# A matmul of zeros ahead of each visit's wait, taken out of the prologue of a graph network kernel

## The reference, cut to what matters

```python
def rgcn_conv(x, src, dst, etype, W, root, bias):      # layer 0, three times
    n = x.shape[0]
    seg = dst * R + etype                              # R = 5 relations
    agg = segment_sum(x[src], seg, n * R)
    cnt = segment_sum(ones, seg, n * R)
    agg = where(cnt > 0, agg / maximum(cnt, 1), 0).reshape(n, R, -1)
    return einsum('nrd,rdk->nk', agg, W) + x @ root + bias

# layer 1 (attention): sums of exp(-leaky_relu(s1[src] + s2[dst])) * h[dst] by src
# layer 2: sums of edge_weight * x[src] by dst, then a linear map
# layer 3: mean of edge_attr by dst, then an MLP
```

## Time and profile before

| | |
|---|---|
| median of 3 runs | 5415.35 us (5401.39 to 5419.33) |
| profiled execution | 5398.16 us |
| its span, first to last instruction | 5396.4 us |
| mean granted TensorE clock | 0.794 |
| TensorE matmuls busy | 3765.6 us (70%) |
| VectorE busy | 2663.4 us (49%) |
| GpSimd busy | 2356.5 us (44%) |
| ScalarE busy | 1163.5 us (22%) |

### The profile page before, as it was taken

One profiled execution on the slowest core, in us unless ns is written; L12 is line 12 of the kernel. 1 busy time (PEld: TensorE's weight loads), 2 busy tenths in 40 slices (PEclk: granted clock), 3 DMA queues, 4 the chain that ended last, 5 costly groups with the idle time before them and its releaser, 6 DMA issues.

```text
span 5396.4 us, 103191 instructions
## 1 busy us (share of the span) xinstructions
PE 3765.6 (70%) x20688; PEld 3046.7 (56%) x20691; DVE 2663.4 (49%) x6964; ACT 1163.5 (22%) x3868; POOL 2356.5 (44%) x2346
## 2 busy tenths in 40 slices
PE   4777677788888766666666776767676766757873
PEld 1333566666666655555555555656565655656762
DVE  7654454444444455545544544444444444892235
ACT  0122111121222111111222222222222222441112
POOL 0000465555555454545555555556555553003430
PEclk8999788888889877766766667887777776888886
DMA  2022333444444322222222223333333432436640
GB/s 73 32 66 75 103 108 114 117 120 118 119 126 133 110 55 55 55 58 64 76 76 74 77 82 104 109 109 108 104 105 107 111 107 67 170 134 176 179 118 12
DMA packets 478385, 526.90 MB, mean 98 GB/s; under 512 B 96596, under 2 KB 398238, under 8 KB 474670
## 3 DMA queue, kind: packets, MB, share of 16 engines
q1 hardware_dynamic: 252780, 246.52, 14.7%
q0 software_dynamic: 85824, 199.51, 13.8%
q10 hardware_dynamic: 139746, 80.46, 5.1%
HBM read 399.82 MB, written 126.39 MB: 98 GB/s over the span
## 4 chain that ended last, share of the span: by engine, by line
PE 31%; issue 25%; DMA 9%; DVE 9%; another core or an unknown queue 7%; POOL 6%; ACTq 4%; ACT 3%; DVEq 3%; SPq 2%; POOLq 1%
DMA msg_r<-y_tab,idx_r 7%; PE psum L1616 6%; POOL msg_r L635 6%; PE psum L1894 3%; PE psum L1689 2%; PE psum L1618 2%; PE psum L1804 1%; DVE shot_r L1151 1%; PE psum L1765 1%; PE psum L1805 1%; DVE h_t L1413 1%; ACT idx_r L712 1%; PE psum L1554 1%; PE psum L1542 1%
## 5 line engine op out<-in xcount | busy, mean ns | idle before, releaser
L635 POOL DMA_INDIRECT msg_r<-y_tab,idx_r x2160 | 2198.1, 1018 | 2327.9 <-issue 1115.5
L1616 PE MATMUL psum<-shot_r 128*128 128x200 f32 x2604 | 982.1, 478 | 404.8 <-issue 207.7
L1145 DVE SCALAR_TENSOR_TENSOR shot_r<-edge_f,win_base,iota 128x600 bf16<-128x600 f32 x434 | 366.3, 844 | 1437.3 <-remote 849.4
L712 ACT COPY idx_r<-row_i 128x1 int32 x2142 | 396.0, 191 | 1921.3 <-DMA msg_r<-y_tab,idx_r 1092.7
L1616 PEld LDWEIGHTS psum<-shot_r 128*128 128x128 f32 x2604 | 542.0, 258 | 438.4 <-issue 433.6
L1689 PE MATMUL psum<-hot_r,msg_r 128*128 128x128 f32 x2880 | 510.4, 320 | 162.1 <-DMA msg_r<-y_tab,idx_r 134.9
L1804 PE MATMUL psum<-msg_r,shot_r 128*128 128x128 f32 x1440 | 394.1, 364 | 305.4 <-DMA msg_r<-in_attr 103.7
L1689 PEld LDWEIGHTS psum<-hot_r,msg_r 128*128 128x128 f32 x2880 | 420.8, 219 | 231.4 <-DMA msg_r<-y_tab,idx_r 143.7
L1131 DVE TENSOR_SCALAR hot_r<-iota,edge_g 128x128 f32<-128x128 f32 x1602 | 446.4, 354 | 181.4 <-PE psum L1805 90.3
L1618 PEld LDWEIGHTS psum<-shot_r 128*100 128x100 bf16 x2604 | 430.2, 165 | 128.6 <-issue 20.3
L1804 PEld LDWEIGHTS psum<-msg_r,shot_r 128*128 128x128 f32 x1440 | 279.1, 241 | 375.2 <-issue 183.2
(11 more groups left out here) (315 smaller groups left out, 4746.5 us busy)
## 6 DMA issues: line engine op xcount, KB each, us to landing
msg_r<-in_attr SPq DMA_DIRECT2D x882, 64.0 KB
h_t<-count_tab SPq DMA_DIRECT2D x25, 1600.0 KB, 6.7
w_tab<-shot_r ACTq DMA_DIRECT2D x385, 100.0 KB
count_tab<-shot_r ACTq DMA_DIRECT2D x385, 100.0 KB
h_t<-w_tab SPq DMA_DIRECT2D x24, 1600.0 KB
msg_r<-y_tab,idx_r POOLq DMA_INDIRECT x2160
xn<-heavy_tab SPq DMA_DIRECT2D x76, 320.0 KB
y_tab<-y_s SPq DMA_DIRECT2D x25, 640.0 KB, 2.9
```

What stands on the lines that cost most here:

```text
L635: pool.indirect_dma_start(out=msg_r[:, q, 0:width], out_offset=None, in_=table, in_offset=bass.IndirectOffsetOnAxis(ap=idx_r[:, q:q + 1], ...
L712: nc.scalar.copy(idx_r[:, q:q + 1], of[:, q:q + COLS - U + 1][:, bass.ds(c0, 1)]).then_inc(s_idx[k], 1)
L1145: V.scalar_tensor_tensor(out=key_b, in0=of(KEY, KW), scalar=win_base[:, bass.ds(w, 1)], in1=to(KW), op0=ALU.subtract, op1=ALU.is_equal).th ...
L1616: T.matmul(win_ps, low_f[:, i, :], weighted_f[:, i, :], start=False, stop=False)
```

## The change

The one line in the visit loop that multiplies zeros into the open sums is taken out. It stood ahead of the wait and added 128 x 128 zeros by 500 columns of zeros to the sums of the window, so the result is unchanged. The opening and the closing matmul of each window stay.

```diff
                     clear(window)
                     with pe.Fori(v0, v1) as v:
                         slot = bounded(pe.snap(v % VD), 0, VD - 1, "it is a remainder")
-                        T.matmul(window, zeros_b[:, 0:P], zeros_b[:, 0:KEYS], start=False, stop=False)
                         pe.wait_ge(s_vis, v)
                         T.matmul(window, visit_r[:, bass.ds(slot, 1), 0:P].rearrange("p o n -> p (o n)"),
                                  visit_r[:, bass.ds(slot, 1), P:P + KEYS].rearrange("p o n -> p (o n)"),
                                  start=False, stop=False).then_inc(s_vfree, 1)
```

## The result

| | before | changed |
|---|---|---|
| median | 5402.92 us (19 runs) | 5450.51 us (19 runs) |
| ratio, 95% interval | | 1.0083 [1.0062, 1.0104] |
| profiled execution | 5398.16 us | 5475.73 us |
| prologue, L1542 of tile 0 to the transposition of the inverse counts | 455.3 us | 498.7 us |
| granted clock in it | 0.93 | 0.71 |

One of the 19 runs of the changed kernel took 5609.29 us at a mean clock of 0.595; it belongs to a slower state of the chip and is left out of the ratio.

What follows compares the result with a forecast made beforehand. TensorE's instruction issue was taken to bound the edited prologue's visits, VectorE those of window 0. Saving 3.2 us and losing 41.8 us in tables gave +38.6 us on 5415.35, so 5454 us; range 5426 to 5474.

Steps and rivals of the forecast that it cites:

- The issue price: Visit loop: each removed load and matmul of zeros saves 0.02 us of TensorE's queue, 3.2 us over 162 visits.
- The upper bound of 0.17: Visit loop: the most a visit could save, 0.32 us between loads less two address instructions; at most 27.5 us in all.
- Window 0: First window's 29 visits: VectorE's one-hot builds set the pace, 0.98 us a visit, so removal saves nothing there.
- The clock: Visits without zeros lose the full clock and nothing restores it before the next table; visits at half clock lose nothing.
- Rival A: Prologue: the clock stays up without the zeros, only the issue is saved, 5412 us; chance 0.10.
- Rival C: Prologue: the clock is lost in only some tiles, half the tables pay, +18 us, 5433 us; chance 0.10.
- The price of a table: Tables at each tile's start: 22 that start at full clock today each lose 1.9 us, 41.8 us in all.
- The upper bound of 2.40: Most a table could lose, in us, from tile 0's 5.36 us table, taken as wholly at half clock, against 2.96.
- The upper end of the sum, +53: Whole kernel: largest loss forecast, 22 tables at 2.40 us each; it gave 5468 us.
- The mean clock of the prologue: Prologue: the mean granted clock was to fall from 0.93 to about 0.65.
- What lies on the path: Prologue: slower tables lengthen their tiles unabsorbed, argued from tile 11 against 12: 2.77 us expected, 2.67 seen.
- The rule that spoke for the change: Skill page blames mid-kernel clock drops on long idle gaps; no visit gap grows long, so the clock would stay up.

## Why the prediction was right

The forecast was a loss of 38.6 us and 5454 us; measured were 48 us by the medians (42 on another chip) and 5450.51 us. That the total is off by only 3.5 us is partly luck: the forecast stood on 5415.35 us, the median of three runs, while 19 runs of the kernel before give 5402.92. The base was 12.4 us too high and the loss 9 us too low. The mechanism is what the runs bear out: the clock is lost, the visits do not pay, the tables do.

- *The issue price.* 0.02 us a visit was taken. The mean distance of visits behind window 0 went from 0.767 to 0.749 us, 0.018 less; the median went from 0.774 to 0.734. Over the 131 distances inside windows that is 2.4 us, against 3.2 forecast. The upper bound of 0.17 was far off, as the doubled zeros show. That 0.02 fits so well is in part luck: it was read from the overlap of two weight loads, and a pair cost 0.006 us with doubled zeros and 0.025 with 8 columns.
- *Window 0.* It saves nothing, as said: a visit every 0.979 us at its end, before and after.
- *The clock.* It was down at the tables, as read off the comparison with the count loop. By the clock in the trace of the changed kernel, 17 of the 24 tables follow a fall between the opening of the window and the table. Ahead of six (tiles 1 to 5 and 11) it had fallen already before the window opened, and the visits did not bring it back; tile 23's table started at full clock and lost it 0.7 us in. Rival A, the clock stays up, is out: 8 columns instead of 500 give the whole loss. Rival C, only some tiles pay, is out for this change, since all 24 tables are slow; it is what 250 columns do.
- *The price of a table.* This term was sized a little low. 1.9 us was taken, on the ground that the table would bring the clock back before or soon after its end. It did, but late: 3.1 to 6.2 us after the table's start. So the mean table took 5.03 us, 2.07 over a fast one. The upper bound of 2.40 was read wrongly: tile 0's table of 5.36 us was not wholly at half clock (its mean was 0.55), and the slowest tables of the changed kernel, tiles 6 and 13, took 5.70, 2.74 over a fast one. With 22 x 1.9 = 41.8 replaced by 24 x (5.03 - 3.10) = 46.3, less the visits' 2.4, the sum is 43.9, against 43.4 us measured. The upper end of the sum, +53, also left out the 3.2 us saved; with them it is +50.
- *The mean clock of the prologue* was guessed at 0.65 and is 0.71: behind every table the clock is up through the small matmuls and the first count groups, which the guess left out.
- *What lies on the path.* That the tables pay and nothing else does was argued from one tile. The sum over all tables shows it (45.9 us more, 2.5 less elsewhere), and the kernels without f32 table matmuls bear it out: 43.4 us of difference become -1.0.
- *The rule that spoke for the change.* The Trainium skill, "TensorE: Matmul & The Clock Gate", "Why this matters for your kernels", lays a fall of the clock in mid-kernel to long idle gaps. The trace showed a fall in count loops without such a gap, and the changed kernel shows it in the visits: TensorE starts a matmul every 0.74 to 1.02 us there and is kept at half clock (0.50 from 114 to 137 us, PE busy 15.70 of 23). The measurement decides.

What stays open is a small effect in the passes. The 34 us between the two first profiles are no sign of one, as single executions of the same passes lie 35 us apart. But the loss by the interval, 33 to 56 us, less the prologue's 43.4, leaves anything from -10 to +13 us there.

## What to carry to other kernels

In this kernel a matmul of zeros in a loop that is bound by its own instructions was nearly free and still paid, because a dense f32 burst follows; before taking such a line out, look for the next burst and read its time in a place where the clock was down. Look at what the engine runs at in the burst, from its start to its end, not at the mean clock: zeros in the count loop raised the mean and bought nothing, and some slow tables began at full clock. And where a loop repeats at the pace of its instruction stream, price an edit by what it does to that stream: the time in flight of what is removed, here 71 us, said nothing of the 2.4 us saved.

## What the runs showed of the hardware

- The number of matmuls did not hold the clock: with 191 zeros matmuls of 8 columns it was 0.69 in the prologue, with 250 columns 0.83, with 500 columns 0.92 to 0.93, with two of 500 0.95.
- TensorE's clock can be lost in steady work. The changed kernel's window 0 starts a 500-column matmul every 0.74 to 1.02 us and was kept at 0.50 for 23 us, with PE busy 15.70 us of it. The busy share of a profile does not tell the clock, as a matmul is longer in flight at half clock (596 against 382 ns).
- The clock can fall just as dense work starts. Before the change tile 11's table, at 338.92 us, took 4.65 us instead of 2.96, though the clock had been 1.00 from 336 to 338.9 us; in the table it was 0.63.
- A pair of weight load and matmul more or less changed this loop by 0.006 to 0.025 us a visit: three 500-column matmuls fit in a visit of 0.76 us where one takes 0.73.
